# Whole-array attention with keys laid out in blocks, fed by DMAs

## The reference, cut to what matters

```
mod = silu(c) @ wmod                               # six rows per entry
h = layernorm(x) * (1 + ca) + sa
q, k, v = h @ W* + b*                              # 16 heads of 8
q, k = rope(q), rope(k)
scores = where(causal, q @ k.T / sqrt(8), -inf)    # per head 256 x 256
attn = softmax(scores) @ v
x = x + ga * (attn @ Wo + bo)
h = layernorm(x) * (1 + cb) + sb
x = x + gb * moe(h)                                # top 2 of 8 experts, gelu, 128 -> 512 -> 128
```

## Time and profile before

| what | value |
|---|---|
| median of three runs | 774.05 us (770.82 to 779.35) |
| profiled execution | 777.98 us, of it 776.2 us span |
| mean granted TensorE clock | 0.719 of 2.4 GHz |
| busy: PE, DVE, ACT, POOL | 610.2, 443.2, 364.6, 355.9 us |

### The profile page before, as it was taken

The page is one execution under the profiler, slowest core; times in us unless marked ns, Lnnn a source line. Parts: engine busy times, 40 slices in busy tenths (PEclk is TensorE's granted clock), DMA queues, the critical chain, the costliest instruction groups (busy, mean ns, idle before and its releaser), DMA issues.

```text
span 776.2 us, 15198 instructions
## 1 busy us (share of the span) xinstructions
PE 610.2 (79%) x4224; PEld 450.2 (58%) x4224; DVE 443.2 (57%) x1882; ACT 364.6 (47%) x1003; POOL 355.9 (46%) x515
## 2 busy tenths in 40 slices
PE   1589898898899889888986667586698787899960
PEld 1355665565655555656554444354488677798960
DVE  2367657647465585575696838270356644467753
ACT  0234553553544535545433434243376655677740
POOL 2223344343242442442523665645335477755552
PEclk9755866755655666666565858565599999999985
DMA  3833199000000000000000000100112122233433
GB/s 100 268 114 125 42 130 126 15 8 8 7 7 14 7 7 14 5 9 7 7 15 4 26 31 18 32 18 27 28 36 55 46 74 69 73 83 99 141 87 118
DMA packets 48560, 40.70 MB, mean 52 GB/s; under 512 B 6347, under 2 KB 44756, under 8 KB 48257
## 3 DMA queue, kind: packets, MB, share of 16 engines
q1 hardware_dynamic: 43968, 31.68, 18.6%
q0 software_dynamic: 4544, 8.47, 3.3%
HBM read 24.35 MB, written 16.69 MB: 53 GB/s over the span
## 4 chain that ended last, share of the span: by engine, by line
PE 54%; DVE 15%; POOL 10%; issue 9%; DMA 7%; ACT 3%; DVEq 1%; SPq 1%; POOLq 0%; ACTq 0%
PE ps_pv L1327 9%; PE misc L1270 8%; PE ps_sc L1310 5%; PE misc L1378 5%; PE ps_max L1292 5%; DVE ps_max L1074 4%; POOL sorted_rows L537 4%; PE ps_sc L1218 4%; PE misc L1349 3%; DMA results<-qkv,probs 3%; PE ps_max L1225 2%; DMA probs<-sorted_rows 2%; PE ps_max L1294 2%; POOL probs L575 2%; PE ps_pv L1225 2%
## 5 line engine op out<-in xcount | busy, mean ns | idle before, releaser
L1074 DVE CUSTOM_DVE_ANT_0 ps_max<-ps_max,mask_q 128x128 f32<-128x128 f32 (+1 forms) x512 | 166.4, 389 | 79.2 <-PE ps_max L1294 79.0
L743 ACT ACTIVATE probs<-ps_sc 128x384 f32<-128x384 f32 x256 | 121.8, 490 | 184.3 <-PE ps_sc L1312 183.1
L575 POOL TENSOR_SCALAR_AFFINE_SELECT probs<-probs 128x512 f32<-128x512 f32 x128 | 81.8, 641 | 167.5 <-ACT probs L743 167.4
L1327 PE MATMUL ps_pv<-probs,v_wides 128*32 128x256 f32 (+1 forms) x1024 | 87.1, 483 | 29.5 <-POOL probs L575 29.4
L546 POOL DMA_INDIRECT results<-qkv,probs x78 | 79.3, 1017 | 67.6 <-DVE qkv L891 54.3
L1310 PE MATMUL ps_sc<-qm_stack,k_stacks 26*128 26x256 f32 x256 | 104.0, 480 | 2.5 <-ACT probs L743 2.5
L702 ACT ACTIVATE early_a<-ps_sc,v_wides 128x128 f32<-128x128 f32 x312 | 98.4, 373 | 3.2 <-PE ps_sc L1218 2.7
L1218 PE MATMUL ps_sc<-x_in,v_wides 128*128 128x128 f32 x624 | 87.3, 285 | 6.9 <-DVE probs L883 6.6
L1218 PEld LDWEIGHTS ps_sc<-x_in,v_wides 128*128 128x128 f32 x624 | 78.1, 197 | 10.1 <-issue 9.6
L1292 PEld LDWEIGHTS ps_max<-k_stacks,q_stack 24*128 24x128 f32 x256 | 39.0, 239 | 67.1 <-DVE maxima L1074 41.3
L1327 PEld LDWEIGHTS ps_pv<-probs,v_wides 128*32 128x32 f32 x1024 | 35.7, 147 | 68.0 <-POOL probs L575 29.4
(11 more groups left out here) (135 smaller groups left out, 1034.5 us busy)
## 6 DMA issues: line engine op xcount, KB each, us to landing
sorted_rows<-blank_s SPq DMA_DIRECT2D x1, 5070.0 KB, 42.5
probs<-sorted_rows SPq DMA_DIRECT2D x78, 65.0 KB, 1.9
gates<-gate_rows SPq DMA_DIRECT2D x1, 4096.0 KB, 12.5
x_in<-in_x SPq DMA_DIRECT2D x16, 128.0 KB, 2.1
x_res<-in_x SPq DMA_DIRECT2D x16, 128.0 KB, 2.1
wfc_s<-in_w_fc SPq DMA_DIRECT2D x1, 2048.0 KB, 9.3
wproj_s<-in_w_proj SPq DMA_DIRECT2D x1, 2048.0 KB, 8.8
heads_ts<-results SPq DMA_DIRECT2D x8, 256.0 KB, 3.1
```

Source lines behind the costliest of these rows:

```text
L575: nc.gpsimd.affine_select(two, two, [[0, 2], [0, 2], [1, P]], ALU.is_ge, 0.0, base=0, channel_multiplier=-1).then_inc(S["causal_done"], 1)
L743: nc.scalar.activation(probs[:, h % 8, :], ps_sc[h % 2][:, 0:384], ACT.Exp, scale=SCALE).then_inc(S["exp_done"], 1)
L1074: last = nc.vector.tensor_tensor_reduce(ps_max[h % 3][:, a * P:a * P + n], ps_max[h % 3][:, a * P:a * P + n], mask_q[:, T - n:T], 1.0, MASKED,
L1327: last = nc.tensor.matmul(ps_pv[rows, a * P:T], vw[:, a, h, :], probs[:, h % 8, :].rearrange("p (c q) -> p c q", q=P)[:, a:3:2, :], start= ...
```

## The change

The attention half is rebuilt; the expert half keeps its work. The change, in words:

- A step has 12 slots (`UNITS`): a unit is a third of a group of four heads. In unit c = 0 of a group all four heads' first 128 queries against the first 128 keys; in c = 1 and 2 two heads' later 128 queries against all 256 keys.
- The keys of each head lie in their own block of columns (`k_diag`: 128 rows, group, head, 256), zero in the rows of the group's other heads, so that one product over all 128 rows serves several heads. A maximum product has 512 columns. The products for the exponentials also run over all 128 rows.
- Everything is computed transposed: `qk` and `rot` are products with permuted weights (`wqk_s`), q and k on the partitions and tokens along the columns; `rot` gives the rotated partner. DVE adds bias and multiplies with the transposed rope tables (`turn_with`), POOL sums (`rope_sum`), ACT writes the high part, DVE the low part, of q and k together.
- The spreads by transposes are gone. `stack_rows` on SP copies the high and low parts into the stacks by 24 DMAs of 8 partitions and two of zeros, and waits first for the low part of the next entry and for the last scores of the previous one.
- The negative maxima of a group are transposed (`sh0` to `sh3`), copied out by ACT, and put into rows 24 and 25 of the queries by four DMAs per group (`shift_rows`).
- The mask and the maximum stay one DVE instruction per head and half (`maxima_of`).
- `LAG = 7`: the exponentials of unit n - 7 run in slot n, so that scores of group 0 start in slot 7 of the same step, those of group 1 in slot 10, of group 2 in slot 1 and of group 3 in slot 4 of the next.
- At the start there are sixteen permuting copies, eight transposes, larger memsets, and eight DMAs of ones. There is one step more ahead (t = -2); the expert tiles begin in slot 1 of the last step, 11 of them within it. Gate rows are loaded entry by entry.

The diff, cut to its core:

```diff
+UNITS = 3 * GROUPS
+LAG = 7
...
 USES = {
-    -1: [('qm0', -1), ('qm1', -1)],
-    1: [('heads0', -2), ('heads1', -2)],
-    3: [('k0', 0), ('q0', 0), ('k1', 0)],
-    4: [('attnT', -2)],
-    5: [('q1', 0)],
-    7: [('wo', -2), ('zT', 1)],
-    8: [('qkv0', 1)],
-    9: [('qkv1', 1)],
-    12: [('z2T', -2)],
-    14: [('router', -2)],
+    0: [('zT', 1), ('attnT', -2)],
+    1: [('sh3', -1), ('qk', 1)],
+    2: [('rot', 1)],
+    3: [('wo', -2)],
+    4: [('sh0', 0)],
+    7: [('sh1', 0), ('z2T', -2)],
+    9: [('router', -2), ('v', 1)],
+    10: [('sh2', 0), ('heads0', -1), ('heads1', -1)],
 }
 MISC = [use for slot in sorted(USES) for use in USES[slot]]
-RESIDUAL_AT, QKV_AT, NORMALISE_AT = 7, (7, 8), 10
-TILES_AT = max(slot for slot in USES for name, _ in USES[slot] if name == "heads1") + 1
-TILES_IN = HEADS - TILES_AT
+assert len(MISC) % 2 == 0
+RESIDUAL_AT, NORMALISE_AT, LOGITS_AT = 4, 6, 9
+TILES_AT = 1
+TILES_IN = UNITS - TILES_AT
...
-MAX_AT = {5: (0, 1,), 6: (2, 3,), 7: (4, 5,), 8: (6, 7,), 9: (8, 9,), 10: (10, 11,), 11: (12, 13,), 12: (14, 15,)}
+PV_AT = {11: (0, 0), 2: (1, -1), 5: (2, -1), 8: (3, -1)}
+HEADS_OUT_AT = {0: (0, -1), 3: (1, -1), 6: (2, -1), 9: (3, -1)}
+SHIFT_AT = {2: 0, 5: 1, 8: 2, 11: 3}
+SELECT_AT = {9: (0, 0, 0), 10: (0, 1, 0), 0: (1, 0, -1), 1: (1, 1, -1), 3: (2, 0, -1), 4: (2, 1, -1), 6: (3, 0, -1), 7: (3, 1, -1)}
+def exp_unit(n):
+    return ((n - LAG) % UNITS, -1 if n < LAG else 0)
+STACKED = 16 * (4 * 6 + 2)
+SHIFTED = 16 * 4
...
+                def shift_rows(g, d):
+                    if s.has(d):
+                        s.wait(sp, S["shift_out"], d, 4, g + 1)
+                        for part in range(2):
+                            for a in range(TILES):
+                                at = (a * 2 + part) * 4
+                                sp.dma_start(part_rows(q_stack[(s.t + d) % 2], part)[:, g, a * P:(a + 1) * P],
+                                             shift_t[g % 2][at:at + 4, :].bitcast(F32)).then_inc(S["shift_in"], 16)
+                def stack_rows():
+                    if not s.has(1):
+                        return
+                    s.hold(sp, S["low_done"], 1, 1, 1, S["sp_passed"])
+                    s.hold(sp, S["score_mm"], -1, UNITS, UNITS, S["sp_passed"])
+                    n = (s.t + 1) % 2
+                    for w in range(4):
+                        for j, part in enumerate((high, low, high)):
+                            at = ROWS * w + DK * j
+                            sp.dma_start(k_diag[n][at:at + DK, :, w, :].bitcast(F32), part[ROWS * w:ROWS * (w + 1), 1, :].bitcast(F32)).then_inc(S["stacked"], 16)
+                        for j, part in enumerate((high, high, low)):
+                            at = ROWS * w + DK * j
+                            sp.dma_start(q_stack[n][at:at + DK, :, :].bitcast(F32), part[ROWS * w:ROWS * (w + 1), 0, :].bitcast(F32)).then_inc(S["stacked"], 16)
+                    for part in range(2):
+                        sp.dma_start(part_rows(q_stack[n], part), zero_row[:].bitcast(F32).rearrange("p (o t) -> p o t", o=1).broadcast_to([4, GROUPS, T])
+                                     ).then_inc(S["stacked"], 16)
+                shift_rows(3, -1)
+                shift_rows(0, 0)
+                stack_rows()
+                shift_rows(1, 0)
+                shift_rows(2, 0)
...
+                def rope_sum():
+                    if s.has(1):
+                        s.hold(pool, S["rot_turned"], 1, 2, 2, S["pool_passed"])
+                        s.hold(pool, S["low_done"], 0, 1, 1, S["pool_passed"])
+                        nc.gpsimd.tensor_tensor(roped[:], turned_a[:], turned_b[:], ALU.add).then_inc(S["roped_done"], 1)
...
+                def high_part():
+                    s.wait(act_e, S["roped_done"], 1, 1, 1)
+                    s.wait(act_e, S["stacked"], 0, STACKED, STACKED)
+                    nc.scalar.activation(high[:].rearrange("p c t -> p (c t)"), roped[:], ACT.Copy).then_inc(S["high_done"], 1)
...
+                def turn_with(name, dst, at, sem_name):
+                    bank = misc[BANK[name]]
+                    s.wait(dve, S[f"{name}_mm"], 1, 1, 1)
+                    s.wait(dve, S["roped_done"], 0, 1, 1)
+                    if s.t == -1:
+                        dve.wait_ge(S["tables_done"], 2)
+                    for n in range(2):
+                        nc.vector.scalar_tensor_tensor(
+                            out=dst[:, n * T:(n + 1) * T], in0=bank[:, n * T:(n + 1) * T], scalar=bias_t[:, at + n:at + n + 1],
+                            in1=rope_t[:, at // 2, :], op0=ALU.add, op1=ALU.mult).then_inc(S[sem_name], 1)
+                def low_part():
+                    s.wait(dve, S["high_done"], 1, 1, 1)
+                    nc.vector.tensor_tensor(low[:].rearrange("p c t -> p (c t)"), roped[:],
+                                            high[:].bitcast(F32).rearrange("p c t -> p (c t)"), ALU.subtract).then_inc(S["low_done"], 1)
...
+                def maxima_of(m):
+                    g, c = divmod(m, 3)
+                    s.hold(dve, S["max_mm"], 0, UNITS, m + 1, S["dve_passed"])
+                    keys, a, first = (P, 0, 4 * g) if c == 0 else (T, 1, 4 * g + 2 * (c - 1))
+                    for n in range(512 // keys):
+                        of = ps_max[m % 3][:, n * keys:(n + 1) * keys]
+                        last = nc.vector.tensor_tensor_reduce(of, of, mask_q[:, T - keys:T], 1.0, MASKED,
+                                                              ALU.add, ALU.max, maxima[:, a, first + n:first + n + 1])
                     last.then_inc(S["max_done"], 1)
...
+                def shift(g):
+                    s.wait(dve, S["max_done"], 0, UNITS, 3 * g + 3)
+                    if g >= 2:
+                        s.hold(dve, S["shift_tr"], 0, 4, g - 1, S["dve_passed"])
+                    else:
+                        s.hold(dve, S["shift_tr"], -1, 4, g + 3, S["dve_passed"])
+                    if s.t == 0 and g == 0:
+                        dve.wait_ge(S["zeroed"], 8)
+                    m = maxima[:, :, 4 * g:4 * g + 4]
+                    v = shifts[:, g % 2, 0:16].rearrange("p (a f w) -> p a f w", a=TILES, f=2)
+                    nc.vector.tensor_scalar(v[:, :, 0], m, -1.0, None, ALU.mult).then_inc(S["shift_high"], 1)
+                    s.wait(dve, S["shift_high"], 0, 4, g + 1)
+                    nc.vector.scalar_tensor_tensor(out=v[:, :, 1], in0=m, scalar=-1.0, in1=v[:, :, 0].bitcast(F32),
+                                                   op0=ALU.mult, op1=ALU.subtract).then_inc(S["shifts_done"], 1)
...
+                def scores_for_max(m):
+                    g, c = divmod(m, 3)
+                    if m >= 3:
+                        s.wait(pe, S["max_done"], 0, UNITS, m - 2)
+                    else:
+                        s.wait(pe, S["max_done"], -1, UNITS, UNITS + m - 2)
+                    if s.t == 0 and m == 0:
                         pe.wait_ge(S["mod_done"], 4)
                         pe.wait_ge(S["size_done"], 1)
                         pe.wait_ge(S["gate_done"], 3)
...
+                        pe.wait_ge(S["zeroed"], 9)
+                        pe.wait_ge(S["ones_in"], 128)
+                    if m == 0:
+                        s.wait(pe, S["stacked"], 0, STACKED, STACKED)
+                    q, ks = q_stack[s.t % 2], k_diag[s.t % 2]
+                    bank = ps_max[m % 3]
+                    if c == 0:
+                        nc.tensor.matmul(bank[:].rearrange("p (w k) -> p w k", w=4), q[:, g, 0:P], ks[:, g, :, 0:P],
+                                         start=True, stop=True).then_inc(S["max_mm"], 1)
                     else:
...
+                        w = 2 * (c - 1)
+                        nc.tensor.matmul(bank[:], q[:, g, P:T], ks[:, g, w:w + 2, :].rearrange("p w k -> p (w k)"),
...
+                def scores(u, d):
+                    g, c = divmod(u, 3)
+                    if c == 0:
+                        s.wait(pe, S["shift_in"], d, 4 * SHIFTED, SHIFTED * (g + 1))
+                    if u >= 2:
+                        s.wait(pe, S["exp_done"], d, UNITS, u - 1)
+                    else:
+                        s.wait(pe, S["exp_done"], d - 1, UNITS, UNITS + u - 1)
+                    if s.t == 0 and u < 2:
+                        pe.wait_ge(S["tables_done"], 2)
+                    q, ks = q_stack[(s.t + d) % 2], k_diag[(s.t + d) % 2]
+                    bank = ps_sc[u % 2]
+                    if c < 2:
+                        for n in range(2):
+                            last = nc.tensor.matmul(bank[:, n * T:(n + 1) * T], ks[:, g, 2 * c + n, 0:P], q[:, g, :],
+                                                    start=True, stop=True)
+                    else:
+                        for w in range(4):
+                            last = nc.tensor.matmul(bank[:, w * P:(w + 1) * P], ks[:, g, w, P:T], q[:, g, P:T],
```

(58 more changed lines are left out.)

585 lines of the change are left out of this document (250 added, 335 removed), and 3 rows, old and new, of the table freed.

## The result

The changed kernel takes **1079.45 us** (median of four runs, 1076.73 to 1084.46) against 776.33 of the kernel before beside it: **1.392 times** as long, 95% interval 1.382 to 1.403. A kernel's executions can fall into a slower state, over 1.5% above its fastest one: ratios are of the fast ones, which are all four here, two of four in x9, and one of four, not the profiled one, in x11. The forecast was 982, its range up to 1070; the median lies 9 us above the range. The profiled execution has 1082.7 us of span and 1084.46 in all.

What follows compares the result with a forecast made beforehand. TensorE's queue bounds the kernel before, 30.6 us a step. Changed, a 29.0 us walk plus 15.5 of issues and landing makes 44.5; over 14 periods plus ends the expert tiles start 207.5 later: 774 + 207.5 = 982 us, range 870 to 1070.

Steps and rivals of the forecast that it cites:

- the loop low_done, stack, shift, scores(3): Attention step: scores(3) waits for group 1's shift, queued behind 26 stack DMAs that wait for low_done; period 44.5 us against 30.6.
- issue doesn't bind: Rival: small DMAs issue fast enough for the slots of cover, leaving TensorE's +3.8 us; period 34, 822 us, chance 0.08.
- The price of an issue: SyncE's queue: each stack or shift DMA issue taken at 0.47 us from the loads, 0.41 low end, 0.7 high.
- the term had 15.5: From low_done to scores(3): 29 issues at 0.47 make 13.6, landing 1.7, semaphores 0.2, together 15.5 us.
- the 14 periods: Repeats of the loop between the first scores(3), step 0, and the last that waits for a stack, step 14; 44.5 us each.
- The walk of 29.0 us: TensorE and VectorE work from scores(3) to the next low_done: 33.8 us at low clock, 25.0 at high, 29.0 taken.
- The ends: Attention stage's start and end: first scores(3) at 77 us, 54 after the last looped one, 12 kept for routing and sorting.
- TensorE's +3.8 us a step: TensorE at low clock: −5.4 spreads, +1.0 shift transposes, +2.8 projection, +5.4 maximum products make +3.8 us of work.
- The single price: TensorE: one 512-column maximum product costs 0.54 to 0.59 us at the low clock, about half at the high one.
- VectorE, ScalarE, GpSimd at nothing: Per step VectorE about +0.3 us, ScalarE −3, GpSimd loses four operations; no effect on the time by themselves.
- The two rivals on the clock: Faster: issues don't bind and TensorE's clock is higher, 724 us, chance 0.04; worse: 0.7 issues, low clock throughout, 1128, 0.06.
- The page's rule: Skill page on DMA issuing: several issuing engines save only small sequencer time; by it the stack would cost one latency.

Runs made afterwards that it cites:

- x9: Changed kernel with group 1's shift ahead of the stack, blank-row write and keys' twelve stack DMAs on ScalarE's queue, three each in slots 7 to 10: 896.3 us.
- x11: Kernel before the change, with both maximum products of each head issued twice into the same bank: median 824.0 us against 789.8.
- x1: Changed kernel with group 1's shift rows issued ahead of the 26 stack DMAs instead of behind them: 994.3 us, ratio 1.280.
- x2: Changed kernel with only the first two heads of each group stacked, 12 stack DMAs instead of 24: 959.3 us, ratio 1.218.
- x4: Changed kernel with none of the 24 stack DMAs, every other instruction kept: 866.4 us, ratio 1.100.
- x6: Kernel before the change, with 33 SBUF to SBUF copies of eleven shapes, three of each, at its very end: one run, 818.7 us.
- x5: Changed kernel with the 5 MB write of blank rows issued on ScalarE's queue instead of SyncE's: 1045.5 us, ratio 1.345.
- x7: Changed kernel with the keys' twelve stack DMAs issued on ScalarE's queue in its slot 7: 985.3 us, ratio 1.251.
- x8: Changed kernel with group 1's shift ahead of the stack, blank-row write and keys' twelve stack DMAs (all in slot 7) on ScalarE's queue: 928.8 us, ratio 1.180.
- x10: Changed kernel without its 24 stack DMAs and with each 512-column maximum product issued twice into its bank: 896.4 us, ratio 1.135.

## Why the prediction was right in kind and short in size

- **Direction, place and loop: right.** The stack issues delay group 1's shift, scores(3) waits, and the wait is in the loop low_done, stack, shift, scores(3). x1, x2 and x4 each took part of it away and got it back. TensorE's gap ahead of scores(3) is 16.1 us where I named about 8: 6.5 of the difference is the price of the issues. Of the rivals, "issue doesn't bind" is excluded, and x4, which makes it true, bears its price out: 866.4 less the 34 of the long step is 832, or 817 with the expert stage of the main run, against 822.
- **The price of an issue: the step that failed**, "I take 0.47, with 0.41 as the low end and 0.7 as the high one". It is 0.72 from one to the next: low_done to scores(3) takes 22.0 where the term had 15.5, +6.5 a step. The rows showed loads only, and I took the common one; the eleven shapes of copy from SBUF to SBUF cost 0.58 to 0.77 (x6), and the 0.7 that I kept as the high end was the price. It is +90 us over the 14 periods and +12 ahead of them: by itself it takes 982 to some 1084, an estimate from these sums.
- **The walk of 29.0 us** measured 28.0 in the mean of the ten steps from 315.3 us on, at a granted clock of 0.65: −1.0; in the first three steps it is 4.5 less. With the 21.9 from low_done to scores(3) the mean step is 50.0, against 44.5.
- **The blank rows were not in the sum.** I had found SyncE's queue in order, and costed what the change puts on it, but not what already lay on it: the 5 MB write of step 3, which in the kernel before had only loads behind it. Its trace had the sign, 15.62 us for one load. +36 us in one step; x5 shows the cause.
- **The ends.** First low_done 33.9 (predicted 34), first maximum 54.1 (48.5), first scores(3) 89.0 (77), +12, again issues. From the last looped scores(3), 814.2, to the expert tiles 52.4 against 66: routing and sorting disappear in the wait more than I kept. So 866.6 − 766 = +12 + 102 − 13.6, where the 102 are the 14 periods: +90 issues, +36 blank rows, −24 walks. Expert stage 216.1 (218). That the median is only 9 us above the range is luck: the blank rows, left out, and the walks and ends, taken too long, cancel.
- **TensorE's +3.8 us a step: an amount without its cause.** The step without the stack is 4.5 longer than before, as if that term held, but TensorE is busy 24.0 us in it, against 27.1 before and 24.9 in the changed kernel. Its busy spans, each weighted with its granted clock, make 33.4 us of low clock a step before, 32.4 in the changed kernel and 32.3 in x4 (an estimate from the traces): the added work isn't there. The single price was right at the low clock (0.55, forecast 0.54 to 0.59) and over half of it at the high one (0.34). What the rebuilt step costs is TensorE's waiting for VectorE, 11 us a step in x4. In the full kernel 9 us of these waits stand in the walk, which had such waits in it; they don't hide behind the issues but add to them.
- **VectorE, ScalarE, GpSimd at nothing:** right in this kernel, where they idle more than half of each step. The two rivals on the clock did not come: 0.65 against 0.63.
- **The page's rule.** The Trainium skill (DMA: Bandwidth & Descriptors, Issuing engines are not separate DMA queues) calls the sequencer's time "usually small relative to the DMA itself". Here 26 issues take 18.8 us against a landing of 1.5, and a second engine issuing 12 of them takes the ratio from 1.392 to 1.251 (x7): in a chain of small DMAs the measurement decides against it.

What stays open: how much of TensorE's waiting in x4 comes from the maxima's length and how much from the order of slots (a kernel with another order was not tried), why the blank rows cost nothing more in x5 but 11 and 22 us in x8 and x9, and why an issue from SBUF to SBUF costs half as much again as a load.

## What to carry to other kernels

Before many small DMAs replace work on an engine, multiply their number by the issue price of their own kind (0.7 us here, whatever the bytes) and find who waits behind the last of them; a short DMA that is urgent goes ahead of the batch, and the batch is dealt over two engines in portions that fit between their own instructions. When a queue gets new, urgent members, read what else lies on it over the whole run: one large write ahead of them cost 36 us. An amount that comes out right is no evidence for its cause: only doubling the one engine's work and shortening the other's, read with busy times and the clock, showed that both count.

## What the runs showed of the hardware that I had not expected

- Issue of a DMA from SBUF to SBUF: 0.58 to 0.77 us on SyncE for blocks of 4 to 128 partitions and 4 to 128 KB (x6), 0.50 for the shifts' 2 KB, against 0.37 to 0.47 for most loads; two engines issuing together pay 0.71 each instead of 0.67.
- The load issued behind a 5 MB write on the same queue held its engine 39.01 us at the issue itself, against 1.64 with the write on another engine's queue (x5). In x9, with the write on the other queue too, it was 9.94.
- Every maximum product repeated in x4 raised the granted clock of its ordinary steps (0.75 in 257 to 433 us of x4, 0.79 in x10), which pays for part of them.
